# Routed token tiles transposed by the DMA crossbar as two planes of 16-bit halves, in place of TensorE's transposes

## The reference

```python
x = x + tanh(g_xattn[0]) * xattn(layernorm(x), ctx_768, ...)   # 16 heads of 64, context of 2 x 64 rows
x = x + tanh(g_ffn[0])   * ffn(layernorm(x), ...)

def ffn(x):                                  # D = 256, H = 512, E = 8 experts, S = 2 shared
    sh = gelu(x @ sw1 + sb1);  shared_out = (sh @ sw2 + sb2.sum(0)) / S
    gates = x @ router_w + router_b
    topv, topi = top_k(gates, 2);  probs = softmax(topv)
    comb = one_hot(topi, E) weighted by probs
    h = gelu(x @ w1[e] + b1[e]);  y[e] = h @ w2[e] + b2[e]
    return shared_out + sum_e comb[:, e] * y[e]
```

## Time and profile before

| | |
|---|---|
| median of 3 runs (range) | 401.89 us (399.97 to 402.12) |
| the profiled execution, and its span | 405.52 us, 403.8 us |
| PE busy | 386.6 us, 96% |
| DVE, ACT, POOL busy | 281.0, 249.4, 218.5 us |
| mean granted clock of TensorE | 0.994 |
| routed stage, from the first w1 products on | from 238.7 us |

### The profile page before, as it was taken

How to read it: one execution, slowest core, us unless ns; L and a number is a source line. 1 busy time by engine, 2 the same in 40 slices (tenths; PEclk the granted TensorE clock), 3 DMA queues, 4 the chain that set the end, 5 groups by cost and what they waited for, 6 DMA issues and landing times.

```text
span 403.8 us, 9115 instructions
## 1 busy us (share of the span) xinstructions
PE 386.6 (96%) x2750; PEld 358.8 (89%) x2751; DVE 281.0 (70%) x611; ACT 249.4 (62%) x601; POOL 218.5 (54%) x260
## 2 busy tenths in 40 slices
PE   8999989999999997898999989999999999999996
PEld 7898879899899887898989978999999999999996
DVE  4798699888888887576677895555455455555386
ACT  3776435646646535765587747666777666667850
POOL 7366566788788755745760044555555555552200
PEclk9999999999999999899999999999999999999999
DMA  8980000000000093005900012222222222221297
GB/s 243 313 265 2 2 13 28 15 26 15 13 26 14 15 339 117 14 3 128 290 4 2 0 41 57 77 80 81 78 78 65 78 78 77 71 75 52 71 356 239
DMA packets 32090, 35.76 MB, mean 89 GB/s; under 512 B 9394, under 2 KB 26108, under 8 KB 32060
## 3 DMA queue, kind: packets, MB, share of 16 engines
q1 hardware_dynamic: 27212, 25.08, 20.3%
q0 software_dynamic: 4768, 10.28, 8.4%
q10 hardware_dynamic: 80, 0.02, 0.0%
HBM read 25.79 MB, written 9.59 MB: 88 GB/s over the span
## 4 chain that ended last, share of the span: by engine, by line
PE 80%; DVE 9%; ACT 4%; issue 3%; POOL 3%; another core or an unknown queue 1%; DVEq 0%; POOLq 0%; ACTq 0%
PE psum L1239 14%; PE psum L1252 13%; PE psum L1050 9%; PE psum L1079 8%; PE psum L1144 8%; PE psum L1113 8%; PE psum L1269 4%; PE psum L1021 3%; PE psum L1228 2%; PE psum L940 2%; PE psum L978 2%; PE psum L1002 2%; POOL half_sum L560 2%; ACT Eb L750 1%; PE psum L921 1%
## 5 line engine op out<-in xcount | busy, mean ns | idle before, releaser
L638 POOL DMA_INDIRECT xsl<-y_rows,table x39 | 38.0, 974 | 58.7 <-issue 27.6
L1716 DVE COPY hs<-psum 128x512 f32<-128x512 f32 x39 | 27.0, 692 | 57.8 <-issue 35.7
L645 POOL DMA_INDIRECT y_tok<-ysl,table x39 | 38.3, 982 | 32.1 <-ACT ysl L883 28.7
L624 POOL DMA_INDIRECT names<-named,pos x32 | 35.6, 1113 | 20.0 <-ACT early_hT_hi L824 11.5
L900 ACT ACTIVATE hr<-psum,b_cur 128x128 f32<-128x128 f32 x156 | 44.2, 371 | 2.0 <-DVE hr_lo L1706 1.2
L883 ACT ACTIVATE ysl<-psum,table 128x256 f32<-128x256 f32 x39 | 18.5, 473 | 38.9 <-PE psum L1239 38.0
L577 POOL TENSOR_TENSOR Eb<-Eb,rinv 128x512 f32<-128x512 f32 x32 | 33.6, 1069 | 8.5 <-DVE rinv L1424 8.5
L779 ACT ACTIVATE yTb<-psum 128x256 f32<-128x256 f32 x16 | 6.2, 385 | 45.0 <-PE psum L1096 45.0
L560 POOL TENSOR_TENSOR half_sum<-Eb 128x512 f32<-128x512 f32 x16 | 20.6, 1289 | 22.9 <-ACT Eb L750 22.9
L820 ACT ACTIVATE early_stage<-psum,vec_col 128x256 f32<-128x256 f32 x48 | 19.8, 465 | 19.8 <-PE psum L1113 16.3
L1252 PE MATMUL psum<-w_hi,xsT_hi 128*128 x78 | 27.6, 435 | 0.7 <-DVE xsT_lo L1700 0.7
(11 more groups left out here) (246 smaller groups left out, 1180.9 us busy)
## 6 DMA issues: line engine op xcount, KB each, us to landing
w_raw<-in_L_ffn_w SPq DMA_DIRECT2D x2, 4096.0 KB, 13.9
y_got<-y_tok SPq DMA_DIRECT2D x8, 512.0 KB, 7.5
xs_all<-in_x SPq DMA_DIRECT2D x4, 512.0 KB, 12.2
sw_raw<-in_L_ffn_sw SPq DMA_DIRECT2D x2, 1024.0 KB, 13.5
y_rows<-ybuf SPq DMA_DIRECT2D x16, 128.0 KB
out<-xs_all SPq DMA_DIRECT2D x3, 512.0 KB, 3.0
wq_sb<-in_L_xattn_Wq SPq DMA_DIRECT2D x2, 512.0 KB, 7.0
wo_sb<-in_L_xattn_Wo SPq DMA_DIRECT2D x1, 1024.0 KB, 15.1
```

The lines of the kernel that those rows point to most:

```text
L624: nc.gpsimd.indirect_dma_start(names, bass.IndirectOffsetOnAxis(ap=pos[:, k, t:t + 1], axis=0), named[:, k, t, :], None).then_inc(scattere ...
L638: nc.gpsimd.indirect_dma_start(xsl[:, s % 2, :], None, y_rows, bass.IndirectOffsetOnAxis(ap=table[:, s, 0:1].bitcast(I32), axis=0)).then_i ...
L645: nc.gpsimd.indirect_dma_start(y_tok, bass.IndirectOffsetOnAxis(ap=table[:, s, 1:2].bitcast(I32), axis=0), ysl[:, s % 2, :], None).then_in ...
```

## The change

The rows of `y_rows` are written as two planes of 16-bit halves (all low halves, then all high halves of the 256 words), so that a gathered tile `xsl` is 128 x 512 elements of 16 bits. ACT makes the planes from `ybuf` in the attention stage (a new operation for each tile, `y_split`). In the routed stage SP issues one crossbar transpose for each slot tile (`dma_start_transpose`, 128 x 512 to four blocks of 128 x 128) into `xsT_planes`, which has one buffer; DVE puts the halves together to words in `xsT` (`words`, one buffer), and signals `xt_psum`; `xsT_hi` and `xsT_lo` are made from `xsT` in SBUF. PE's `turn` is gone. The waits that stood on PE's use of `xsl` now stand on the landing of the crossbar's transposes (`xsl_turned`). Cut to its core, the diff is:

```diff
-        y_rows = nc.dram_tensor("y_rows", [TOK, D], F32, kind="Internal").ap()
+        y_rows = nc.dram_tensor("y_rows", [TOK, 2 * D], U16, kind="Internal").ap()
...
+        y_planes = at_words("y_planes", [P, 2, 2 * D], AT_Y, U16)
...
-        (hs, hr, xsl, xsT_hi, xsT_lo, ysl, hr_hi, hr_lo), end = row_of(AT_STEP, [
-            ("hs", [P, HID], F32), ("hr", [P, HC, P], F32), ("xsl", [P, 2, D], F32),
+        (hs, hr, xsl, xsT_planes, xsT, xsT_hi, xsT_lo, ysl, hr_hi, hr_lo), end = row_of(AT_STEP, [
+            ("hs", [P, HID], F32), ("hr", [P, HC, P], F32), ("xsl", [P, 2, 2 * D], U16), ("xsT_planes", [P, 2, KD, P], U16), ("xsT", [P, KD, P], F32),
...
-                sp.wait_ge(y_ready, t + 1)
-                sp.dma_start(y_row_tiles[t], ybuf[:, t % 2, :]).then_inc(y_kept[t % 2], 16)
+                sp.wait_ge(y_split, t + 1)
+                sp.dma_start(y_row_tiles[t], y_planes[:, t % 2, :]).then_inc(y_kept[t % 2], 16)
...
+            def turn(s):
+                if s == 0:
+                    sp.wait_ge(pairs_used, 2)
+                    sp.wait_ge(sh_lo, (EARLY - 1) * PAIRS + 2)
+                sp.wait_ge(xsl_loaded[s % 2], 16 * (s // 2 + 1))
+                if s >= 1:
+                    sp.wait_ge(xt_psum, s)
+                sp.dma_start_transpose(xsT_planes[:, :, :, :].rearrange("p h k n -> p (h k) n"),
+                                       xsl[:, s % 2, :]).then_inc(xsl_turned[s % 2], 16)
             for s in range(SLOT_TILES):
                 n = s % IN_FLIGHT
                 if s >= IN_FLIGHT:
@@ -459,6 +474,10 @@
                 row = sp.snap(regs[n], min_val=0, max_val=NAME_TILES - 1)
                 sp.dma_start(table[:, s, :], name_tiles[at(row)].rearrange("a p c -> p (a c)")
                              ).then_inc(table_loaded[n], 16)
+                if s >= IN_FLIGHT - 1:
+                    turn(s - (IN_FLIGHT - 1))
+            for s in range(SLOT_TILES - (IN_FLIGHT - 1), SLOT_TILES):
+                turn(s)
...
-                    pool.wait_ge(xt_psum, s - 1)
+                    pool.wait_ge(xsl_turned[s % 2], 16 * (s // 2))
...
+                    if fixed is None or i >= 3:
+                        act.wait_ge(y_kept[q], tiles_before(i - 1, q))
+                    nc.scalar.activation(y_planes[:, q, :].rearrange("p (h d) -> p h d", h=2),
+                                         ybuf[:, q, :].bitcast(U16).rearrange("p (d h) -> p h d", h=2), ACT.Copy
+                                         ).then_inc(y_split, 1)
...
             def turned(s, par):
 
                 act.wait_ge(xt_psum, s + 1)
-                nc.scalar.activation(xsT_hi[:, :, :], bank[par][:, 0:D].rearrange("p (k n) -> p k n", k=KD), ACT.Copy
+                if not peeled(s) or s >= 1:
+                    act.wait_ge(h_psum, s)
+                nc.scalar.activation(xsT_hi[:, :, :], xsT[:, :, :], ACT.Copy
                                      ).then_inc(xt_hi, 1)
 
...
-                    if j == 0 and middle:
-                        used.then_inc(first_pair_used, 1)
+                    if j < 3 and signal:
+                        used.then_inc(pairs_used, 1)
...
-            def turn(s, par):
-                pe.wait_ge(xsl_loaded[par], tiles_before(s, par) + 16)
-                if not peeled(s) or s >= 2:
-                    pe.wait_ge(xt_lo, s - 1)
-                for k in range(KD):
-                    last = nc.tensor.transpose(bank[par][:, k * P:(k + 1) * P], xsl[:, par, k * P:(k + 1) * P], ident[:, :])
-                last.then_inc(xt_psum, 1)
...
-                    turn(s + 1, 1 - par)
...
+            def words(s, par):
+                if not peeled(s) or s >= 1:
+                    dve.wait_ge(xt_lo, s)
+                dve.wait_ge(xsl_turned[par], tiles_before(s, par) + 16)
+                nc.vector.tensor_copy(xsT[:, :, :].rearrange("p k n -> p (k n)").bitcast(U16).rearrange("p (k n h) -> p h k n", k=KD, h=2), xsT_planes[:, :, :, :]
+                                      ).then_inc(xt_psum, 1)
             def turned(s, par):
 
                 dve.wait_ge(xt_hi, s + 1)
-                nc.vector.tensor_tensor(xsT_lo[:, :, :], bank[par][:, 0:D].rearrange("p (k n) -> p k n", k=KD),
+                nc.vector.tensor_tensor(xsT_lo[:, :, :], xsT[:, :, :],
                                         xsT_hi[:, :, :].bitcast(F32), ALU.subtract).then_inc(xt_lo, 1)
 
             def hidden_left(s, par):
@@ -1719,12 +1742,16 @@
                     turned(s + 1, 1 - par)
                 if not peeled(s) or s >= 1:
                     hidden_left(s - 1, 1 - par)
+                if not peeled(s) or s + 2 < SLOT_TILES:
+                    words(s + 2, par)
                 if peeled(s) and s + 1 == SLOT_TILES:
                     columns_rest(EARLY, late)
 
             expert, fetch = experts(dve)
             fetch(0, 0)
+            words(0, 0)
             turned(0, 0)
+            words(1, 1)
             w2_rest(7)
             add_step(EARLY - 1)
             routed(dve, step, {1: lambda: w2_rest(0)})
```

More of the change, by code:

```diff
@@ L20 @@
 U32 = mybir.dt.uint32
+U16 = mybir.dt.uint16
 ALU = mybir.AluOpType
@@ L274, in build @@
             sem(n) for n in ("route", "chosen_ready", "count_psum", "dif_ready", "ex_ready", "pos_ready", "routed_all"))
-        first_pair_used = sem("first_pair_used")
+        pairs_used, y_split = sem("pairs_used"), sem("y_split")
+        xsl_turned = [sem(f"xsl_turned{i}") for i in range(2)]
         cols_hi, cols_ready, comb_ready, ct_psum, bias_hi, cur_ready, sh_psum, sh_raw, sh_hi, sh_lo, acc_psum, acc_free = (
@@ L904, in step @@
                 nc.scalar.activation(hr_hi[:, par, :, :], hr[:, :, :], ACT.Copy).then_inc(ht_hi, 1)
-            act.wait_ge(sh_lo, (EARLY - 1) * PAIRS + 2)
+            act.wait_ge(sh_lo, (EARLY - 1) * PAIRS + 3)
+            act.wait_ge(pairs_used, 3)
             turned(0, 0)
@@ L1134, in later_biases, with project @@
                 last.then_inc(bias_psum, 1)
-            def project(c, buffers, with_bias=True, with_later=False, middle=None, acc=ACC, bias=None):
+            def project(c, buffers, with_bias=True, with_later=False, signal=False, acc=ACC, bias=None):
                 _, _, (hT_h, hT_l) = buffers
@@ L1208, in _, with shared_step @@
             project(1, early, with_bias=False)
-            def shared_step(c, buffers, with_later=False, middle=None):
+            def shared_step(c, buffers, with_later=False, signal=False):
                 hidden(c, buffers, HALVES[0])
@@ L1213, in shared_step @@
                 hidden(c, buffers, HALVES[1])
-                project(c, buffers, with_later=with_later, middle=middle)
+                project(c, buffers, with_later=with_later, signal=signal)
             pe.wait_ge(b2_ready, 1)
@@ L1273, in _ @@
             fetch(0, 0)
-            shared_step(EARLY - 1, early, middle=lambda: turn(0, 0))
+            shared_step(EARLY - 1, early, signal=True)
             pe.wait_ge(w1_ready, E)
```

8 lines of the change are left out of this document (3 added, 5 removed).

## The result

The changed kernel takes 441.29 us (median of 4 runs, 440.59 to 442.82), the kernel before 402.0 us in the same comparison: a ratio of 1.099 (95% interval 1.096 to 1.102), so 39.3 us slower. The direction and the kind of loop are those of the prediction; the loss is 2.1 times the forecast 18.5, though the time lies within the forecast range (397 to 452 us).

A forecast was written before the change was run, and what follows sets the result against it. PE was taken to bound the routed stage at 3.48 us a step; a 3.85 us transpose loop would replace it. 405.5 + 17.0 (routed stage) + 1.5 (attention) = 424.0, less 3.6 to the median: 420.4 us, range 397 to 452.

The forecast's parts named there:

- the pair: PE's two transposes of the next tile's rows per routed step; removal saves 0.22 us, 8.1 us over 37 steps.
- The loop: Routed stage: DVE's copy, SP's waits and table load, crossbar transpose, next copy; 3.85 us a step, so PE waits.
- T: Crossbar transpose of 128 KB from issue to landing; 2.35 us, the middle of plain transfers of 2.1 and 2.6.
- R: Round trip from the transpose's issue to DVE's next copy: T and the semaphore behind it; 2.40 us counted.
- the copy: DVE's `words` copy of 512 halves in SBUF, one term of the routed step; 0.60 us.
- the way through SP: From the copy's end through SP's table load to the transpose's issue, in each routed step; 0.85 us counted.
- attention: Attention stage: ACT's added operation for each of 16 tiles, mostly hidden; 1.5 us more, 8.5 if nothing covered it.
- The lower bound of 1.7: Shortest transpose time from issue to landing, in us, taken from an indirect load of the same 128 KB.
- The first rival: Routed stage: transfer hidden, PE keeps the bound, if the transpose lands in under 1.8 us; 399.2 or 397.7 us, chance 0.20.
- The third rival: Routed stage: crossbar slower than plain transfers, transpose of 3.1 us or more; 449 to 487 us, chance 0.20.
- my own case: Routed stage bound by the transpose's chain, transpose of 2.1 to 3.1 us; 411 to 449 us, chance 0.50.
- The start: Start of the routed stage: PE begins 1.3 us late, step 1 at 246.1 instead of 241.59; no cost of its own.

The follow-up runs named there:

- Runs 2 to 4: Changed kernel with the transpose issued ahead of the table load, 424.21 us; with a second plane buffer instead, 436.9 us; with both edits, 404.66 us.
- run 7: Changed kernel with each crossbar transpose replaced by a plain copy of the same 128 KB, rows untransposed: 427.07 us, ratio 1.061.
- run 2: Changed kernel with SP issuing each transpose ahead of the table load instead of behind it: 424.21 us, ratio 1.056.
- run 11: Changed kernel with POOL's scatter of each tile issued twice, the extra one to a tensor nothing reads: 465.64 us, ratio 1.140, on a slower chip.
- run 6: Changed kernel with each transpose replaced by a plain 4 KB copy, DVE taking the untransposed gathered rows: 401.85 us, ratio 1.001.

## Why the prediction was right and where it was wrong

**The bound, right.** The kernel before was bound by PE in this stage. Without the pair and without a transfer the middle steps take 3.29 us, where 3.26 was forecast, so the pair was worth 0.19 us a step and not 0.22. (That the mean period of the copies is 3.26 is chance: the first two copies lie 1.47 us apart, since PE doesn't pace them.) The kernel gained 6.4 us for the forecast 8.1.

**The loop, right.** PE waits at L1284 (ahead of L1268 only at its first product), DVE ahead of each copy, SP for DVE's copy and not for a gather. Runs 2 to 4 show it by its parts: the loop opens only when both of SP's waits for the one count go. A second buffer by itself is worth 4 us, since the table load holds the queue.

**The size of a term, wrong: "The middle is 2.35"**, the transpose's T. Its mean over the stage (tiles 1 to 38) is 3.04, and R, for which 2.40 was counted (0.05 of the 0.1 for semaphores belongs there), is 3.10. It is nearly the whole error:

- loop: 38 x (4.43 - 3.85) = +22.0 us. In it, a step, R is +0.70, the copy -0.14 (0.46 for 0.60), and the way through SP +0.02 (0.87 for 0.85).
- attention: 0 for 1.5, so -1.5.
- rest: +0.4, which is what remains and not a measured row. The sum is 420.4 + 22.0 - 1.5 + 0.4 = 441.3.

The 0.69 us by which T was missed have two parts, by run 7. A plain transfer of the same 128 KB in this place landed in 2.66 us as a mean, so the middle of the two plain rows was 0.31 too low for this place; the crossbar's form adds 0.38. The two rows weren't alike in what was beside them: the 128 KB stores of `out` were issued at the end of the program among other stores (the engines are nine tenths busy there), the 96 KB load was one of the first of the program, and neither goes from SBUF to SBUF. The lower bound of 1.7 was too low for another reason: it took the end of the bytes for the landing. In the last, quiet transpose the bytes end 1.94 us behind the issue and the landing comes at 2.41.

Where the 0.70 us of R come from in time, as far as runs and rows show:

- A quiet transpose takes what I forecast. The last one of the changed kernel, when POOL has no gather left, is issued at 399.88 and the copy starts at 402.31: 2.43 us. The landing's minimum is 2.4. That this agrees with 2.35 is luck: a plain transfer of the same size took 1.98 in the same place.
- In the middle of the stage it is 2.86, so 0.4 more. The 128 KB plain copy grows too, from 1.98 (last tile) and 2.30 (first) to 2.65; the 4 KB copy less, from 1.69 and 1.88 to 1.86. With the gather issued at the same time it is 3.30 (run 2). So it reads as large transfers in the same stretch that lengthen each other, though the engines' mean share is 0.37; run 11 leans that way.
- The rest, 0.2 us as a mean over all steps, lies in single long round trips: tiles 36 and 37 (4.68 and 4.27, with the gather at the same moment), the start of the stage (3.09 and 3.33 for tiles 1 and 2), and tiles 6 and 9 (4.49 and 4.16), which have beside them a 16 KB load of instructions. The trace of 258 to 264 us holds the transpose of tile 6, issued at 258.54 and landed 4.4 us later: busy tenths of the DMA engines and what they moved, in 40 slices, then the queue of the instruction load.

```profile
DMA  0000000228937899990900000000790000000000
GB/s 0 0 0 0 0 0 0 5 5 164 164 82 306 256 352 263 181 225 0 27 0 0 0 7 9 10 9 10 231 437 0 0 0 0 0 0 0 0 0 0
...
q8 instruction: 1, 0.02, 1.3%
```

A slice is 0.15 us. From 261.0 to 262.2 us the engines' share is under a tenth, while the transpose is open; the last of the bytes come at 262.2 to 262.5, and the copy started at 263.03. The trickle of 7 to 10 GB/s in this gap is the transpose itself: by the single packets of the trace, the 16 KB of instructions were under way from 260.25 to 261.50, and from 261.48 on pieces of 256 bytes of the transpose went one after the other until 262.3, when all else that was open ended too. It looks as if the instruction load held one of the engines and the others waited for that engine's share. No run took the instruction load away, so this is read, not shown.

**The crossbar itself, smaller than its form suggests.** Against a plain copy of the same bytes R is 0.21 us longer in the middle, 0.38 as a mean over the stage (3.10 against 2.72), and the whole kernel 14 us slower (427.1 to 441.3; 38 x 0.38 is 14), of 46 us that the transfer costs. The page "VectorE: DVE Perf Modes" (The three transpose paths) of the Trainium skill gives 1309 ns for a block of 128x128. Four times that, an estimate, would have been 5.2 us; the quiet transfer took 2.43 for all four, so the figure doesn't add up block by block. The Trainium skill's page "Advanced Engine Details and Errata" (X-Bar Transpose (TRN2)) says that transposes are as fast as plain transfers. In the middle the runs come near to it, 2.86 against 2.65 us; in the quiet last tile they don't, 2.43 against 1.98, and SP is held for 1.20 us by the issue instead of 0.47. This long issue was one of the prediction's signs of being wrong; it lies within R and isn't a term of its own.

**The rivals.** The first rival's point of decision was right: at an R of 1.86 the middle steps run at PE's pace and the kernel is even with the one before (run 6). That T would be so short was wrong, and its lower bound of 1.7 isn't reached by any transfer of 128 KB in this place. The third rival's threshold, a T of 3.1, was just missed: T's mean is 3.04, its median in the middle 2.8, and ten of the 39 transposes are above 3.1. So 441 us falls into my own case (T from 2.1 to 3.1, 411 to 449), at its slow end. POOL's issue didn't hold the copy: the copy lasts 451 to 491 ns in all 39 steps, since in this order POOL starts its gather 0.65 us behind the copy's start.

**The start, right in form.** `hs` of step 0 stands behind `words(1)` and `w2_rest` and starts at 241.08 us, 2.46 behind the start of `words(1)`. What I did not count is the clock: after PE's first wait of 3.13 us it was at its lower level from 236.6 to 250.3 us, and again from 263.9 to 267.3.

## What to carry to other kernels

A transfer in a chain counts with its whole round trip in each step, here some 1.9 us with almost nothing in it and 2.0 to 3.3 with 128 KB; before moving work from a busy engine to a DMA, open the chain, with every wait of the issuing queue (also those of unrelated loads ahead of it) and every buffer one tile further. A single buffer or a single reordering may show little, since two locks hold the same door; here 4, 17 and, together, 37 us. Take the duration of a transfer from rows with the same kind of neighbours, source and destination, not from a quiet stretch, and not from the end of its bytes but from its landing. Even then the best that could be had was a part of the small saving on the engine that was unloaded: 2 us of 402.

## What the runs showed of the hardware that I had not expected

- A crossbar transpose's issue holds SP's queue for 1.20 us, for 128 KB and for 64 KB alike (1205 and 1184 ns), a plain one for 0.47.
- From SBUF to SBUF 128 KB land in 2.0 us at best and 2.6 beside a gather and a scatter; the stores of 128 KB to memory in the attention stage landed in 1.7.
- DVE's `ybuf` over 128x256 words lasted 0.35 or 1.28 us, by 0.07 us in its start against POOL's products.
- Beside a gather and a scatter, the last bytes of a 128 KB transfer between SBUF buffers moved 0.5 us (crossbar) and 0.35 us (plain) before its landing, as medians of the middle steps.
